# Attention scores of a row tile made in one group of eight products over four PE row groups, the second tile's moved behind the down projection

## What is computed

```python
q, k, v = proj(query, Wq, bq), proj(key, Wk, bk), proj(value, Wv, bv)   # 16 heads of 16 features
scores = jnp.einsum('bhqd,bhkd->bhqk', q, k) / math.sqrt(D_K)
p_attn = jax.nn.softmax(scores, axis=-1)
x = jnp.einsum('bhqk,bhkd->bhqd', p_attn, v)
...
return x @ Wo + bo
```

## Time and profile before

| what | us |
|---|---|
| median of 3 runs | 1871.33 (1869.11 to 1872.06) |
| span of the profiled execution | 1868.3 |
| PE busy | 1319.0 (71%) |
| DVE busy | 1255.1 (67%) |
| POOL busy | 1008.7 (54%) |
| ACT busy | 834.4 (45%) |

### The profile page before, as it was taken

How to read it: one execution, slowest core, us unless ns; L and a number is a source line. 1 busy time by engine, 2 the same in 40 slices (tenths; PEclk the granted TensorE clock), 3 DMA queues, 4 the chain that set the end, 5 groups by cost and what they waited for, 6 DMA issues and landing times. The chain is left out here.

```text
span 1868.3 us, 32990 instructions
## 1 busy us (share of the span) xinstructions
PE 1319.0 (71%) x8936; PEld 1144.7 (61%) x8937; DVE 1255.1 (67%) x3313; ACT 834.4 (45%) x2767; POOL 1008.7 (54%) x1250
## 2 busy tenths in 40 slices
PE   6604558700036676766765899998489999999997
PEld 4403446500024455655654778877389999999997
DVE  4499999999988999999876144454434444443442
ACT  5522224501103666666866488887323322322332
POOL 3258998887669999998866425342111122122121
PEclk9857778955567887878867999998689999999999
DMA  4611113540031000100102212133130410411200
GB/s 117 204 40 35 47 41 112 175 125 0 17 125 38 23 28 23 33 27 27 28 28 79 62 35 59 50 124 115 45 102 21 147 55 20 154 48 45 77 17 7
DMA packets 108409, 119.22 MB, mean 64 GB/s; under 512 B 22769, under 2 KB 87720, under 8 KB 106280
## 3 DMA queue, kind: packets, MB, share of 16 engines
q1 hardware_dynamic: 70760, 90.98, 15.6%
q10 hardware_dynamic: 33136, 18.58, 3.4%
q0 software_dynamic: 4432, 8.73, 1.4%
HBM read 83.44 MB, written 35.74 MB: 64 GB/s over the span
## 5 line engine op out<-in xcount | busy, mean ns | idle before, releaser
L242 POOL TENSOR_TENSOR wt<-wt 128x1024 f32<-128x1024 f32 x128 | 301.3, 2354 | 47.1 <-DVE wt L187 32.2
L248 POOL TENSOR_TENSOR wt<-wt 128x512 f32<-128x512 f32 (+2 forms) x384 | 306.8, 799 | 30.1
L1902 PE MATMUL e_ph<-e_g,e_w 128*128 128x128 f32 x2496 | 285.2, 275 | 0.7 <-ACT e_g L1872 0.7
L1902 PEld LDWEIGHTS e_ph<-e_g,e_w 128*128 128x128 f32 x2496 | 281.9, 192 | 0.9 <-issue 0.9
L187 DVE SCALAR_TENSOR_TENSOR wt<-wt,scan 128x256 f32<-128x256 f32 x512 | 244.8, 478 | 1.8 <-POOL wt L242 1.8
L166 DVE TENSOR_REDUCE wt<-wt 128x16 f32<-128x272 f32 x512 | 222.2, 434 | 0.1
L177 DVE TENSOR_TENSOR scan<-wt,scan 128x256 f32<-128x256 f32 x512 | 217.8, 425 | 0.3
L155 DVE TENSOR_TENSOR wt<-wt,scan 128x256 f32<-128x256 f32 x512 | 213.0, 416 | 0.5 <-PEq L265 0.5
L1380 ACT ACTIVATE wt<-p_pX,p_mx 128x120 f32<-128x120 f32 x512 | 176.4, 387 | 71.7 <-DVE p_mx L1165 71.5
L1781 POOL TENSOR_TENSOR e_ve<-e_mv,eps 128x1 f32<-128x1 f32 x39 | 7.4, 189 | 330.9 <-DVE e_mv L1837 330.9
L1863 ACT ACTIVATE e_g<-e_ph,wt 128x128 f32<-128x128 f32 x156 | 48.7, 363 | 304.9 <-PE e_ph L1902 304.9
(11 more groups left out here) (226 smaller groups left out, 2814.5 us busy)
## 6 DMA issues: line engine op xcount, KB each, us to landing
wt<-in_L_ffn_W SPq DMA_DIRECT2D x24, 1024.0 KB, 5.2
qkv<-f_st ACTq DMA_DIRECT2D x48, 256.0 KB, 2.3
p_kE<-kE SPq DMA_DIRECT2D x16, 480.0 KB, 3.8
p_vP<-vP SPq DMA_DIRECT2D x16, 480.0 KB, 4.5
wt<-qkv SPq DMA_DIRECT2D x6, 1024.0 KB, 9.9
e_xt<-routed ACTq DMA_DIRECT2D x39, 130.0 KB, 2.1
f_xt<-in_x SPq DMA_DIRECT2D x16, 256.0 KB, 2.8
p_oT<-o SPq DMA_DIRECT2D x16, 256.0 KB, 2.9
```

What stands on the lines that cost most here:

```text
L242: nc.gpsimd.tensor_tensor(x, s["S"][:, h, z * Q:(z + 1) * Q], s["qn"][:, h, z * Q:(z + 1) * Q].rearrange("p t (o d) -> p t o d", o=1).to_b ...
L248: nc.gpsimd.tensor_tensor(x[:, :, :, 0:half], x[:, :, :, 0:half], x[:, :, :, half:2 * half], ALU.add).then_inc(s["o_fold"][h], 1)
L1902: ins = nc.tensor.matmul(ph2[:, c // 2, c % 2], w2[:, s, i, c * P:(c + 1) * P], g1[:, i], start=(i == 0), stop=(i == C1 - 1))
```

## The change

`score(c, q)` now makes all eight products of a row tile: for each g all four row groups, each into its own bank. `score_done` still rises twice a tile, behind the last product of the first two row groups and behind that of the other two, so DVE and ACT keep their programs. The first tile's call waits for the last copy of probabilities (PT_out 8) as a whole. The second tile's call waits until both halves of the first tile are exponentiated (`exp_done` 2), and stands behind the second half of the down projection and ahead of the output projection.

```diff
--- before.py
+++ after.py
@@ -1545,21 +1545,20 @@
                         ins = nc.tensor.matmul(pq[:, go], wq[:, g, go * P:(go + 1) * P], x1T[:, g], start=(g == 0), stop=(g == G - 1))
                 ins.then_inc(q_done, 1)
 
-            def score(c, x):
-                q = x // 2
-                if x == 0:
+            def score(c, q):
+
+                if q == 0:
                     pe.wait_ge(q_out, (c + 1) * G)
                     pe.wait_ge(k_in, c * 16 + 16)
-                if x >= 2:
-                    pe.wait_ge(exp_done, c * HALVES + (x - 1))
+                else:
+                    pe.wait_ge(exp_done, c * HALVES + 2)
                 for g in range(G):
-
-                    for i in range(2):
-                        group = x % 2 * 2 + i
+                    for group in range(4):
                         rows = slice(32 * group, 32 * group + 32)
-                        ins = nc.tensor.matmul(pX[:, x % 2, i, g * 2 * CTX:(g + 1) * 2 * CTX], qT[rows, g, q * P:(q + 1) * P],
+                        ins = nc.tensor.matmul(pX[:, group // 2, group % 2, g * 2 * CTX:(g + 1) * 2 * CTX], qT[rows, g, q * P:(q + 1) * P],
                                                kE[rows, q, g].rearrange("p a c -> p (a c)"), start=True, stop=True)
-                ins.then_inc(score_done, 1)
+                        if g == G - 1 and group % 2:
+                            ins.then_inc(score_done, 1)
 
             def probabilities(d, some):
                 for j in some:
@@ -1633,11 +1632,8 @@
                     probabilities(d, range(6, 8))
                 if "c" in on:
                     if "d" in on:
-                        pe.wait_ge(PT_out, d * 8 + 6)
+                        pe.wait_ge(PT_out, d * 8 + 8)
                     score(c, 0)
-                    if "d" in on:
-                        pe.wait_ge(PT_out, d * 8 + 8)
-                    score(c, 1)
                 if "f" in on:
                     if "c" in on:
                         pe.wait_ge(x1T_out, c + 1)
@@ -1648,17 +1644,15 @@
                     down(f, 0)
                 if "d" in on:
                     values(d)
-                if "c" in on:
-                    score(c, 2)
                 if "f" in on:
                     down(f, 1)
+                if "c" in on:
+                    score(c, 1)
                 if since(a, 1) and ("d" in on or "a" in on):
                     pe.wait_ge(hT_done, a * G)
                 if "d" in on:
                     pe.wait_ge(pv_out, d + 1)
                     by_rows(pm, aT, wo, att_done)
-                if "c" in on:
-                    score(c, 3)
                 if "a" in on:
                     pe.wait_ge(o_in, a * 16 + 16)
                     if "d" in on or since(d, 1):
```

## The result

| kernel | median us | runs |
|---|---|---|
| before | 1870.22 | 4 (1868.97 to 1872.06) |
| after | 1903.26 | 4 (1898.34 to 1905.4) |

The changed kernel takes 1.0171 times as long, 95% interval 1.0158 to 1.0183: 33.0 us more. The profiled executions have spans of 1868.3 and 1903.7 us, 35.4 us apart. The forecast was 1899.6 us, with 28.3 us as the sum.

What follows compares the result with a forecast made beforehand. The prediction took a chain through PE, DVE and ACT as the bound. Its terms sum to 28.3 us; on the 1868.3 us span that gives 1896.6, plus 3.0 us between span and median 1899.6 us, range 1885 to 1914.

Steps and rivals of the forecast that it cites:

- The bound: Loop steps 16 to 18: a chain of scores, maxima and exponentials through PE, DVE and ACT sets the time, not PE's work.
- PE's rival: Steps 15 to 20: PE is the bound, merged halves save 0.8 and 1.0 us a step, 11 us, to 1860; chance 0.06.
- First tile, one wait later: Loop step, first tile: all eight products wait for the last copy, so the first maximum starts 0.90 us late; PE gains nothing.
- two halves in a row: Upper bound for eight score products: 2.0 us, twice 1.01 us; the lower bound was 1.08 us and 1.1 us was taken.
- Second tile: Loop step: third maximum 3.7 us later, fourth 3.2 us later through DVE's queue; the step takes 3.2 us more, first tile included.
- Clock: Loop steps: a 3.0 us hole on PE before the mixer's product lowers its clock; 0.5 us a step counted, bounds 0 and 1.8.
- The rival's 1914: Steps 14 to 21: the slower clock after PE's hole puts all 1.8 us a step on the chain, 1914 us; chance 0.09.
- Steps 4 to 7: DVE is full and covers late scores by 1.5 us in step 5, so no cost; only step 4's first maximum adds 0.9 us.
- Steps 8 and 9: Steps with half the scan: the third maximum moves by 2.2 us with no wait behind it, 4.4 us for both.
- Steps 10 to 13: Step 10: PE at the lower clock after a long idle, eight products take about 1.9 us; +2.8 us.
- Steps 14 and 15, 19 to 21: Fourth maximum 1.7 us late in step 14, 2.1 in step 15; 15, 19 and 20 together 6.3 us, step 21 1.1.
- The sum: Whole kernel: loop steps 9.6, steps 15, 19, 20 6.3, steps 14 and 21 2.8, steps 4, 8, 9, 10 8.1, clock 1.5; 28.3 us.

Runs made afterwards that it cites:

- the kernel with the fill: Changed kernel plus six products with unused results on PE, between output projection and mixer's product in steps 14 to 21; 1900.36 us, ratio 1.0158.
- the numbering moved: Changed kernel with the numbering of the rows (L1193, two elements a partition) on POOL instead of DVE; 1899.78 us, ratio 1.0156.

## Why the prediction was right, and where it wasn't

- **The bound.** "A step is one chain through several engines; PE fills the time between its parts." Right: each half of the change alone is slower, though each takes work off PE, and PE's rival (1860) is out.
- **First tile, one wait later.** 0.90 us forecast, 0.97 measured against the head of the step; eight products 1.09 us for the 1.1 taken. The bound of two halves in a row would have been 2.0. That PE gains nothing there held too.
- **Second tile.** Third maximum 3.7 us later, measured 3.72; fourth 3.2, measured 3.10. That DVE's queue decides the fourth is right as a time, but it isn't the link that carries the step alone: with the fourth maximum early the step got longer. Residual, mixer's product and `kept` hang on the same queue.
- **Clock.** 0.5 us per loop step: 0.5 in two of the three, 1.1 in the third; some more in steps 15 and 20, which I had left out. The rival's 1914 counts the sum's 1.5 us a second time; by its own terms it is 1912.5.
- **Steps 4 to 7: "these cost nothing".** This step of the working failed: 3.65 us, 3.04 of them in L1193. The cover of 1.5 us for the scores was there, no maximum of steps 5 to 7 waited. But a delay on DVE is a shift against POOL, which goes its own way through the scan, and one instruction fell into POOL's product. I had looked only at who waits by semaphores. As the kernel before can fall into it too, how much of it each execution pays is partly chance.
- **Steps 8 and 9.** 4.4 forecast, 3.3 measured, but unevenly: 2.9 in step 8 and 0.4 in step 9. The traces say why: the query product ahead of step 10's scores (L1545, 8 records) takes 3.68 us before (976.60) and 1.97 us after (985.72), with a granted clock of 0.50 (972 to 978) and 0.75 (981 to 987) around it, and DVE's wait behind it falls from 5.53 to 3.81 us. So 1.7 us of 2.1 came back by the clock. In the kernel with the fill the product takes 1.97 us too, and step 9 grows by 0.4; with the numbering moved it takes 3.75 us, and step 9 grows by 2.1.
- **Steps 10 to 13.** 2.8 forecast, 4.95 measured in the profiled run; in the traces of the changed kernel with the fill and with the numbering moved, which don't touch these steps' PE work, it is 2.4 and 2.7. The rest, some 2.3 us, comes with a mixer's product in step 11 that took 3.45 us there and 1.99 us in those two, so it goes with this execution's clock.
- **Steps 14 and 15, 19 to 21.** 3.8 forecast for the first two, 5.9 measured; 5.3 for the last three, 4.8 measured. Counted at the fourth maxima (14.97 - 13.26 in step 14, 17.29 - 14.97 in step 15) they are 1.7 and 2.3, for 1.7 and 2.1 forecast: much of the miss is the border, since the first tile's 0.97 us of the next step is counted with it. The reason given for 15, 19 and 20, that the down projection's end sets the scores and the first tile's delay doesn't add to it, held in the kernel with the first tile's part alone.
- **The sum.** 28.3 forecast, 35.4 in the traces. The difference of 7.1 is L1193 (3.04), step 11 (2.3) and smaller terms of both signs, 1.8 together. The medians are 33.0 apart, since the profiled run of the changed kernel was its slowest. That the forecast for the median is only 3.7 us off owes 1.3 us to the 3.0 us added between span and run, where the runs show 1.7; that is luck, and nothing in the sum stands for the 3.04 us of L1193.

## What to carry to other kernels

When a transfer of work to fewer, larger groups saves time on an engine that looks full, first ask for each group when its last input is ready and what stands behind it in the queues of the others; here the merged products were twice as cheap and cost 1.7%. A piece that can start the next link early is worth more than its engine's time, and no other place tried for it was as good. A delay that is covered by waits can still move an instruction of DVE into a long one of POOL; look at the pairs of the two that stand close to each other in time, not only at semaphores.

## What the hardware showed that was not expected

- A DVE instruction of two elements a partition waits for the end of POOL's running product: 1.90 and 1.29 us instead of 0.14, with ends that agree to 0.03 us. A reduction of 128x272 on DVE runs inside the same product at its 0.42 us. And POOL's small ones wait for DVE's normalisation: 2.71 us for 0.71, 2.12 for 0.20.
- Eight fp32 products of 32 rows over four row groups take 1.09 us, four of them over two row groups 1.08 us; behind 2.73 us of idle PE the eight take 1.98 us.
- The same table load of 1.28 us on ACT lies ahead of the awaited maximum in steps that are written out and behind it in a loop's body, where it is on the chain.
- More work made the kernel no slower: six unused products in a hole brought the following one from 3.49 back to 1.97 us.
